# A graph network kernel: the typed tables of its transformer layers as one product per head, with four node types stacked on the partitions

## The reference

```python
def _typed_transform(xh, W, types):
    out = jnp.zeros_like(xh)
    for t in range(W.shape[0]):
        y = jnp.einsum('mhd,hde->mhe', xh, W[t])
        out = jnp.where((types == t)[:, None, None], y, out)
    return out
...
Q = _typed_transform(xh, W_Q[l], node_type)
K = _typed_transform(xh, W_K[l], node_type)
V = _typed_transform(xh, W_V[l], node_type)
q_dst = Q[dst]
kt = _typed_transform(K[src], W_E[l], edge_type)
scores = jnp.sum(q_dst * kt, axis=-1) / scale
scores = scores * mu[l].T[edge_type]
```

## Time and profile before

| | |
|---|---|
| median of 3 runs | 8000.28 us (7995.58 to 8005.35) |
| the profiled execution, its own time | 8003.79 us |
| its span in the trace | 8002.0 us |
| PE busy in the span | 5981.8 us (75%) |
| DVE busy | 5204.0 us (65%) |
| ACT busy | 3151.4 us (39%) |
| POOL busy | 3541.3 us (44%) |
| mean DMA rate | 86 GB/s |

### The profile page before, as it was taken

How to read it: one execution, slowest core, us unless ns; L and a number is a source line. 1 busy time by engine, 2 the same in 40 slices (tenths; PEclk the granted TensorE clock), 3 DMA queues, 4 the chain that set the end, 5 groups by cost and what they waited for, 6 DMA issues and landing times. The chain is left out here.

```text
span 8002.0 us, 138934 instructions
## 1 busy us (share of the span) xinstructions
PE 5981.8 (75%) x30254; PEld 4761.3 (60%) x30255; DVE 5204.0 (65%) x17428; ACT 3151.4 (39%) x10642; POOL 3541.3 (44%) x3878
## 2 busy tenths in 40 slices
PE   2787577678886788497887897886887887937676
PEld 1665466657774566386665785665875665814455
DVE  7664488768887566538997328997338998353323
ACT  0111266646664466235553225553325553300015
POOL 0677366545552477306662006662006663037740
PEclk9999999899997688699998998998999998955678
DMA  1000211222222233326553026553026554023330
GB/s 29 3 3 3 55 48 48 39 74 73 72 74 40 79 102 102 62 101 187 175 177 84 2 94 185 176 174 96 0 89 180 176 177 104 0 82 100 101 68 16
DMA packets 306941, 689.93 MB, mean 86 GB/s; under 512 B 95900, under 2 KB 135510, under 8 KB 306390
## 3 DMA queue, kind: packets, MB, share of 16 engines
q0 software_dynamic: 209536, 581.61, 27.0%
q1 hardware_dynamic: 81264, 98.11, 3.8%
q10 hardware_dynamic: 15846, 7.19, 0.4%
HBM read 605.77 MB, written 80.89 MB: 86 GB/s over the span
## 5 line engine op out<-in xcount | busy, mean ns | idle before, releaser
L943 POOL DMA_INDIRECT arena<-tab_l,idx x2320 | 2203.7, 950 | 1032.6 <-issue 568.4
L1020 PE MATMUL bank<-arena,onehots 128*128 128x264 f32 (+3 forms) x6496 | 1980.6, 436 | 339.0 <-DVE onehots L852 189.4
L981 PE MATMUL bank<-arena,spreads 128*128 x5568 | 1458.6, 370 | 598.0 <-ACT spreads L1034 242.6
L1020 PEld LDWEIGHTS bank<-arena,onehots 128*128 128x128 f32 x6496 | 1312.1, 221 | 673.7 <-DVE onehots L852 211.9
L981 PEld LDWEIGHTS bank<-arena,spreads 128*128 128x128 f32 x5568 | 966.9, 206 | 827.7 <-issue 761.7
L1213 DVE TENSOR_TENSOR acc<-acc,bank 128x264 f32 (+3 forms) x1624 | 654.9, 403 | 498.2 <-PE bank L1020 486.7
L1034 ACT ACTIVATE spreads<-bank 128x256 f32<-128x256 f32 x1392 | 524.2, 377 | 900.6 <-PE bank L969 896.2
L1108 DVE TENSOR_TENSOR arena<-arena,bank 128x512 f32<-128x512 f32 x928 | 629.3, 680 | 265.9 <-ACT stats L1056 146.7
L861 ACT ACTIVATE onehots<-iota_row,slot_loc 128x128 f32<-128x128 f32 x1856 | 632.3, 391 | 28.6 <-PEq L1693 24.2
L943 POOL DMA_INDIRECT arena<-tab_l0b,idx x464 | 441.2, 951 | 374.9 <-ACT arena L1074 235.6
L930 POOL COPY idx<-slot_typed 128x16 int32 (+1 forms) x87 | 17.8, 204 | 1329.0 <-SPq L901 1328.6
(11 more groups left out here) (331 smaller groups left out, 9925.3 us busy)
## 6 DMA issues: line engine op xcount, KB each, us to landing
tab_l<-arena SPq DMA_DIRECT2D x75, 768.0 KB, 3.5
arena<-tab_l,idx POOLq DMA_INDIRECT x2320
arena<-tab_l0a,idx POOLq DMA_INDIRECT x464
arena<-tab_l0b,idx POOLq DMA_INDIRECT x464
rec_dram<-arena POOLq DMA_INDIRECT x417, 2.1
tab_l<-arena SPq DMA_DIRECT2D x25, 132.0 KB, 1.8
tab_l0b<-arena SPq DMA_DIRECT2D x25, 128.0 KB, 1.7
residual<-X SPq DMA_DIRECT2D x1, 3200.0 KB
```

What stands on the lines that cost most here:

```text
L943: pool.indirect_dma_start(out=rows_sb[:, a, t, 0:width], out_offset=None, in_=table[:, :], in_offset=bass.IndirectOffsetOnAxis(ap=idx[:, a ...
L981: mm = pe.matmul(z[x.k % 2][:, t, 0:cw], spreads[:, x.k % 2, t * P:t * P + P], qtab[:, block_no[w % BG], 0:cw], start=True, stop=not gatv2)
L1020: mm = pe.matmul(sums[x.k % 2], onehots[:, x.a, GT * x.k + t, :], rhs, start=t == 0, stop=t == GT - 1)
```

## The change

Per head, the four masked copies of a block's 32 features are written side by side (type, feature), so that one transpose gives 4 types x 32 features on the 128 partitions of one head. The weights are laid out to match: w_all holds for each head the four types' matrices on the partitions, and 160 columns: Q, V, and three times the product of the key matrix and an edge matrix, scaled by mu. One matmul per head with 160 columns then sums over the types and gives Q, V and the three typed keys. The products of key and edge matrices are made once per layer in a block of their own ahead of the loop. The separate step for the keys and the step for the edge types go. Three heads of a block go to one bank, three to the next, two to the third; ACT takes the first bank out, DVE the other two. stage holds V once beside the three key parts, and the store is two transfers: the three key parts, and V, read three times, into the right halves of the three rows. Both count on one semaphore per buffer, and DVE and ACT wait for both of them. The memset covers 768 columns instead of 3840; 21 weight transfers take the place of 33. The loop counts of the semaphores follow.

```diff
--- before.py
+++ after.py
@@ -1656,39 +1656,72 @@
         def typed_tables(l):
-            w_qv = arena[:, 0:2048].rearrange("p (a k c n) -> p a k c n", a=4, k=2, c=2)
-            w_k = arena[:, 2048:3072].rearrange("p (a k n) -> p a k n", a=4, k=2)
-            w_e = arena[:, 3072:3840].rearrange("p (k a n) -> p k a n", k=2, a=3)
+            w_all = arena[:, 0:1280].rearrange("p (h c) -> p h c", h=H)
+            w_k = arena[:, 1280:1536]
+            w_kT = arena[:, 1536:1792].rearrange("p (k n) -> p k n", k=2)
+            w_e = arena[:, 1792:2560].rearrange("p (k a n) -> p k a n", k=2, a=3)
             mu = small[:, 32:56].rearrange("p (h t) -> p t h", t=3)
-            masked_x = flat_oh[:, 0:2048].rearrange("p (a t c) -> p a t c", a=2, t=4)
-            turned_x = flat_oh[:, 2048:4096].rearrange("p (a k t c) -> p a k t c", a=2, k=2, t=4)
+            masked_x = flat_oh[:, 0:2048].rearrange("p (a h t d) -> p a h t d", a=2, h=H, t=4)
+            turned_x = flat_oh[:, 2048:4096].rearrange("p (a h n) -> p a h n", a=2, h=H)
             is_type = stats[:, 0:4 * NT].rearrange("p (t j) -> p t j", t=4)
-            keysT = spreads
+            parts = [stage[:, a, 0:4 * D].rearrange("p (s h e) -> p h s e", s=4, h=H) for a in range(2)]
             def prepare(dve, link):
-                link(dve.memset(arena[:, 0:3840], 0.0))
+                link(dve.memset(arena[:, 1792:2560], 0.0))
                 for t in range(4):
                     link(dve.tensor_scalar(is_type[:, t, :], type_of[:, :], float(t), None, ALU.is_equal))
             vector_phase(prepare)
             pairs = []
+            for t in range(4):
+                q = slice(32 * t, 32 * t + 32)
+                pairs += [(w_all[q, :, 0:32], A["L2_gnn_W_Q"][l, t].rearrange("h d e -> d h e")),
+                          (w_all[q, :, 32:64], A["L2_gnn_W_V"][l, t].rearrange("h d e -> d h e")),
+                          (w_k[q, :].rearrange("p (h e) -> p h e", h=H), A["L2_gnn_W_K"][l, t].rearrange("h d e -> d h e"))]
             for hh in range(4):
                 q = slice(32 * hh, 32 * hh + 32)
                 for k in range(2):
-                    h = 4 * k + hh
-                    pairs += [(w_qv[q, :, k, 0, q], A["L2_gnn_W_Q"][l, :, h].rearrange("a d e -> d a e")),
-                              (w_qv[q, :, k, 1, q], A["L2_gnn_W_V"][l, :, h].rearrange("a d e -> d a e")),
-                              (w_k[q, :, k, q], A["L2_gnn_W_K"][l, :, h].rearrange("a d e -> d a e")),
-                              (w_e[q, k, :, q], A["L2_gnn_W_E"][l, :, h].rearrange("a d e -> d a e"))]
+                    pairs.append((w_e[q, k, :, q], A["L2_gnn_W_E"][l, :, 4 * k + hh].rearrange("a d e -> d a e")))
             mu_ap = A["L2_gnn_mu"]
             pairs.append((small[:, 32:56], bass.AP(tensor=mu_ap.tensor, offset=l * H * 3, ap=[[0, P], [1, 3 * H]])))
             load(*pairs)
-            vector_phase(lambda dve, link: link(dve.tensor_scalar(small[:, 32:56], small[:, 32:56],
-                                                                  float(32.0 ** -0.5), None, ALU.mult)))
-            qv = [PS[2][:, :].rearrange("p (k c n) -> p k c n", k=2, c=2),
-                  PS[3][:, :].rearrange("p (k c n) -> p k c n", k=2, c=2)]
-            kt = [PS[4][:, 0:D], PS[7][:, 0:D]]
-            ke = [PS[5][:, 0:384].rearrange("p (t n) -> p t n", t=3), PS[6][:, 0:384].rearrange("p (t n) -> p t n", t=3)]
+
+
+            with nc.Block() as block:
+                @block.tensor
+                def _(pe):
+                    for k in range(2):
+                        pe.transpose(PS[0][:, k * P:k * P + P], w_k[:, k * P:k * P + P], ident[:, :])\
+                          .then_inc(multiplied.sem, 1)
+                    pe.wait_ge(step.sem, step.at(2))
+                    for k in range(2):
+                        pe.matmul(PS[2 + k][:, 0:384], w_kT[:, k, :], w_e[:, k, :, :].rearrange("p a n -> p (a n)"),
+                                  start=True, stop=True).then_inc(multiplied.sem, 1)
+
+                @block.vector
+                def _(dve):
+                    dve.tensor_scalar(small[:, 32:56], small[:, 32:56], float(32.0 ** -0.5), None, ALU.mult)\
+                       .then_inc(step.sem, 1)
+                    dve.wait_ge(multiplied.sem, multiplied.at(2))
+                    dve.tensor_copy(w_kT, PS[0][:, 0:2 * P].rearrange("p (k n) -> p k n", k=2)).then_inc(step.sem, 1)
+                    dve.wait_ge(step.sem, step.at(1))
+                    dve.wait_ge(multiplied.sem, multiplied.at(4))
+                    for k in range(2):
+                        for t in range(3):
+                            dve.tensor_tensor(w_all[:, 4 * k:4 * k + 4, 64 + 32 * t:96 + 32 * t],
+                                              PS[2 + k][:, t * P:t * P + P].rearrange("p (h e) -> p h e", h=4),
+                                              mu[:, t, 4 * k:4 * k + 4].unsqueeze(2).to_broadcast([P, 4, 32]), ALU.mult)\
+                               .then_inc(step.sem, 1)
+            multiplied.base += 4
+            step.base += 8
+
+            heads = ((0, 3), (3, 6), (6, 8))
+            prod = [[PS[2 + 3 * a + b][:, 0:160 * (h1 - h0)].rearrange("p (h c) -> p h c", c=160)
+                     for b, (h0, h1) in enumerate(heads)] for a in range(2)]
+
+            def wait_both_stored(eng, j, a):
+                if needed(16 * (j - a)):
+                    eng.wait_ge(stored[a].sem, stored[a].at(16 * (j - a)))
             with nc.Block() as block:
                 @block.vector
@@ -1697,29 +1730,22 @@
                         if needed(j - 1):
                             dve.wait_ge(D_["turned"].sem, D_["turned"].at(j - 1))
                         for t in range(4):
...
+                            op = dve.tensor_scalar(masked_x[:, a, :, t, :], X[:, j, :].rearrange("p (h d) -> p h d", h=H),
+                                                   stats[:, ds(t * NT + j, 1)], None, ALU.mult)
                         op.then_inc(D_["in"].sem, 1)
...
-                    sweep(dve, mask, None, queries, keys)
+                    def give(j, a):
+                        dve.wait_ge(D_["product"].sem, D_["product"].at(j + 1))
+                        wait_both_stored(dve, j, a)
+                        for b in (1, 2):
+                            h0, h1 = heads[b]
+                            dve.tensor_copy(qtab[:, j, 32 * h0:32 * h1].rearrange("p (h e) -> p h e", e=32),
+                                            prod[a][b][:, :, 0:32])
+                            op = dve.tensor_copy(parts[a][:, h0:h1, :, :],
+                                                 prod[a][b][:, :, 32:160].rearrange("p h (s e) -> p h s e", s=4))
+                        op.then_inc(D_["dve_out"].sem, 1)
+
+                    sweep(dve, mask, None, give)
                 @block.tensor
                 def _(pe):
@@ -1727,42 +1753,23 @@
                         pe.wait_ge(D_["in"].sem, D_["in"].at(j + 1))
                         if needed(2 * j):
                             pe.wait_ge(D_["turned_sb"].sem, D_["turned_sb"].at(2 * j))
...
+                        for h in range(H):
+                            op = pe.transpose(PS[h // 4][:, h % 4 * P:h % 4 * P + P],
+                                              masked_x[:, a, h, :, :].rearrange("p t d -> p (t d)"), ident[:, :])
                         op.then_inc(D_["turned"].sem, 1)
                     def transform(j, a):
                         pe.wait_ge(D_["turned_sb"].sem, D_["turned_sb"].at(2 * j + 2))
                         if needed(j - 1):
                             pe.wait_ge(D_["dve_out"].sem, D_["dve_out"].at(j - 1))
...
+                            pe.wait_ge(D_["act_out"].sem, D_["act_out"].at(j - 1))
+                        for b, (h0, h1) in enumerate(heads):
+                            for h in range(h0, h1):
+                                op = pe.matmul(prod[a][b][:, h - h0, :], turned_x[:, a, h, :], w_all[:, h, :],
+                                               start=True, stop=True)
                         op.then_inc(D_["product"].sem, 1)
...
-                    sweep(pe, turn, transform, edge_types)
+                    sweep(pe, turn, transform)
                 @block.scalar
                 def _(act):
@@ -1771,45 +1778,42 @@
                         if needed(j - 1):
                             act.wait_ge(D_["product"].sem, D_["product"].at(j - 1))
                         for k in range(2):
...
+                            act.activation(turned_x[:, a, 4 * k:4 * k + 4, :].rearrange("p h n -> p (h n)"), PS[k][:, :],
+                                           ACT.Copy).then_inc(D_["turned_sb"].sem, 1)
+
+                    def give(j, a):
                         act.wait_ge(D_["product"].sem, D_["product"].at(j + 1))
...
-                    sweep(act, turn, keys)
+                        wait_both_stored(act, j, a)
```

(58 more changed lines are left out.)

35 lines of the change are left out of this document (2 added, 33 removed).

## The result

The changed kernel takes 7688.07 us (median of 4 runs, 7675.66 to 7692.41) where the kernel before takes 8002.82 (4 runs, 7995.58 to 8008.28): ratio 0.9605, 95% interval 0.9588 to 0.9621. A later set of 5 runs gave 7684.81 and 0.9601 (0.9588 to 0.9614). The forecast was 7686, its range 7670 to 7744. The profiled execution is the fastest of its four, 7675.66 us with a span of 7673.7.

What follows compares the result with a forecast made beforehand. PE's own work was taken to bound the kernel. Per layer, stage -105.6, memset -2.6, load -2.0 and added block +5.3 gave -104.9 us, -314.7 for three layers: 7686 us, range 7670 to 7744.

Steps and rivals of the forecast that it cites:

- What bounds the kernel, and PE's price: Typed-table stage: PE's own work sets the pace, 7.41 us a block before, 0.87 + 2.21 = 3.08 after.
- The loop over the store: Store, DVE copies and mask, PE transposes, ACT turn and eviction: 9.28 us over three blocks, 3.09 each, level with PE.
- The pace: Time per block in the stage's loop: 3.2 us, low end 3.08, high end 3.65.
- The stage: Typed tables of one layer: 9.15 us start, 76.8 for 24 blocks, 5.5 end; 91.4 against 197.0.
- Ahead of the loop: Preparation before each layer's loop: memset 2.6 us less, load 2.0 less, added block for the matrices' product 5.3 more.
- The load: Weight transfers ahead of the loop, 33 becoming 21: 2.0 us saved a layer, between 0 and 2.8.
- The sum: All terms together, whole kernel: -104.9 us a layer, -314.7 for three layers.
- A: Rival, the two stores of a block land in series: 4.95 us landing, 3.54 a block, 7711 us; chance 0.13.
- B: Rival, DVE's and ACT's copies out of PSUM become the bound: 3.76 us a block, 7726 us; chance 0.09.
- C: Rival, PE falls to the low clock in the loop: 6.16 us a block, 7899 us; chance 0.03.
- D: Rival, broadcast store on few DMA engines: 7852 us on three, 8636 on one; chance 0.03 still faster, 0.02 slower.
- E: Rival, the stage shortens but the edge passes give it back; chance 0.03 together with something unnamed.

Runs made afterwards that it cites:

- the 128-column run: Changed kernel with each product computing 128 columns instead of 160, copies writing as much as before: stages of 90.8, 90.5 and 90.7 us.
- the run with three rounds: Changed kernel with DVE making its four copies three times, twice to unused space: stages of 121.5, 119.6 and 119.6 us.
- the two that were tried alone: Kernel before with V copied once and a second store reading it three times: 197.39, 198.47, 197.29 us stages; or key-edge product made ahead in old layout: 8308 us whole.

## Why the prediction was right, step by step

*What bounds the kernel, and PE's price.* Right. 8 matmuls of 160 columns take 2.17 us from start to start (forecast 2.21) and the transposes 0.87 to 0.88, 3.05 a block (forecast 3.08). The straight line between 128 and 256 columns held.

*The loop over the store.* Right, and the step that mattered: the loop was drawn in the right order and spans three blocks, as the threes of the 128-column run and the mask moved ahead show. Its sum was forecast at 9.28 and measured at 9.43. The terms were off both ways (forecast, then measured): SP's issue 0.26, 0.40; landing with wake 3.7, 3.83; DVE's copies 1.25, 1.11; PE's and ACT's wakes with the transposes 1.11, 1.35; ACT's turn and copies 1.83, 1.61. The pace, 3.2, was taken above both bounds for handoffs that don't fit; measured 3.20 over the first layer. That the two agree so well is in part luck. Two thirds of the blocks stand at the store loop's 3.13, those ahead of the hardware loop at PE's 3.05, and the mean comes to 3.20 through the cold first distance (3.61) and the late store (1.4 us once), which no step had.

*The stage.* 91.4 forecast, 91.2, 92.6 and 91.6 measured. First product done 9.15 after the start, measured 9.07 in the first layer (3394.81 to 3403.88), but 10.5 and 9.5 in the other two: the 0.8 us for its cold part was enough once, and the five other stages of the two profiles took 1.8 to 2.1. The blocks were forecast at 76.8, measured 75.2 (the last product has no transposes before it). The end was forecast at 5.5, measured 7.0: DVE's last copies wait until 3480.62 for the store of two blocks before. The two errors offset each other.

*Ahead of the loop.* The memset is right (3.26 to 0.70). The added block is right: 5.83 us from DVE's first step to the mask in place of 0.70, 5.1 more (forecast 5.3). Its timeline, and the mask behind it:

```profile
3388.98 0.66 PE L1694 MATMUL bank<-ident,arena 128*128 128x128 f32 x2 [73.25 <-PEq L1321]
...
3389.68 0.42 DVE L1706 COPY arena<-bank 128x256 f32<-128x256 f32 x1 [0.52 <-PE bank L1694]
...
3390.16 2.93 PE L1698 MATMUL bank<-arena 128*128 128x384 f32 x4 [0.52 <-DVE arena L1706]
...
3393.20 1.28 DVE L1711 TENSOR_TENSOR arena<-bank,small 128x128 f32<-128x128 f32 x6 [3.10 <-PE bank L1698]
3394.81 2.19 DVE L1733 TENSOR_SCALAR onehots<-X,stats 128x256 f32<-128x256 f32 x8 [0.33 <-PEq L1690]
```

Two products of 384 columns at the low clock are half of it, as counted. The load is the mis-sized term: 3.5 us saved (7.83 from first issue to DVE, 11.35 before), 2.0 forecast with an upper bound of 2.8. The doubled rows per transfer cost next to nothing, as the rate shows: the flow doubles while the issues stay 0.50 us apart (0.47 for the small ones). Narrow windows of the load, the kernel before and then the changed one:

```profile
3390.00:3390.50 0.50, 0.00 (x0) 0.00 (x0) 0.00 (x0) 0.00 (x0) 0.00 (x0) 0.50 0.44 66
```

```profile
3384.00:3384.50 0.50, 0.00 (x0) 0.00 (x0) 0.00 (x0) 0.00 (x0) 0.00 (x0) 0.50 0.91 139
```

Issues paced the load before. The fewer issues saved 2.7 us of the 3.5; the bound left out that the wait behind the last issue would be shorter as well (3.06 us to DVE instead of 3.84). So from the memset to the mask the first layer has 15.7 us instead of 16.6, where some 17 were forecast.

*The sum.* -318.5 us in the three layers, forecast -314.7. The median of the runs moved by 314.8; that this meets the forecast to 0.1 us is luck, since the time outside the layers differs by 10 us and more between executions. "The other stages move by more than 10 us" was a sign of being wrong, and they moved by 9.8 in the profiled execution and by 6.8 the other way in the other; given their spread, that sign was set too near.

*The rivals.* A: the pair lands at 3.83, much nearer to 3.6 than to 4.95. B: copies take 1.11, not 2.5 (the prediction's 3.75 for DVE was also added up wrong: 2.5 and a mask of 1.13 are 3.63); had they been dear, the run with three rounds shows that DVE's sum would have set the pace. C: the clock held 1.00 with PE idle for a quarter of the time, in pieces of 1.05 us. D: while both stores of a block flow, the DMA engines' share is about 1:

```profile
3447.00:3447.25 0.25, 0.25 (x4) 0.25 (x4) 0.25 (x2) 0.25 (x2) 0.00 (x0) 1.00 1.06 365
...
3448.25:3448.50 0.25, 0.25 (x4) 0.19 (x2) 0.06 (x1) 0.00 (x0) 0.00 (x0) 1.00 1.00 352
```

The second row lies in the second store (issued at 3446.07, 786 KB flow in all from 3446.3 to 3448.8): all 16 engines, in rows of 1 KB read three times. By the rule of the Trainium skill, "DMA: Bandwidth & Descriptors", Rules for kernel authors, a broadcast behind the partitions leaves all engines in use; the trace agrees. The same page's fixed 2.0 us per transfer plus bytes at 436 GB/s gives an estimate of 2.9 for 384 KB (Anatomy of one DMA, for another issuing path); measured 2.5 alone. In series the two would be 5.8 by that estimate, and the trace differs: they overlap. The DMA share in the loop's middle was forecast near 0.65 and is 0.72: the measured pace makes 0.66 of it, and the share per byte is 6% higher than before (0.72 at 250 GB/s, 0.28 at 103). E: the stages kept what they gained; what moved elsewhere moves between executions.

## What to carry to other kernels

Count what PE streams: a block-diagonal weight of four 32x32 matrices multiplies three quarters of zeros, and stacking what was four masked inputs on the partitions takes them out. Once the bound shrinks by more than half, draw the loop that closes over each buffer, with every instruction that stands in an engine's queue behind the wait; here a mask behind a copy behind a store cost some 2.7 us a layer, about half of it through a single late store, and one word in the order of steps gave it back. Parts of a change are not to be priced one by one: of the two that were tried alone, one brought nothing and one made the kernel 300 us slower (160 of them PE's work).

## What the hardware showed that I had not expected

- A load of many small transfers was paced by its issues: 0.47 us per transfer and queue for 12 to 16 KB in 96 to 128 rows of 128 bytes, 0.50 for 32 KB in 256; the flow went from 66 to 139 GB/s, and the DMA engines' share from 0.44 to 0.91, so there is little room beyond.
- Near the entrance of the hardware loop PE lost 0.9 to 1.8 us a stage (a distance of 4.46 instead of 3.05 in the first layer). The late part is a store's: 30 of a pair's 32 landings were in time and the last 1.5 us behind them, after a 16 KB packet of the loading of instructions that took 1.31 us. With the mask ahead the landing is as late (1.9 us behind), and PE loses nothing.
- The low clock at the start lasts differently in executions of the same sequence: 4.42 and 2.90 us for the first product. That is up to 1.5 us a layer, and the largest of the three things that make up the stages' spread. Without the idle piece of 2.9 us ahead of the first transposes the product ran at 2.4 GHz in all three layers (2.34 us).
